# Causal attention scores on one core: mask and maximum of the second chunk in one VectorE instruction, normalisation on VectorE

## What is computed

```
x = _layernorm(x + causal attention 0 (x))        # 16 heads of 8
x = _layernorm(x + top-2 of 8 experts (x))        # relu
x = _layernorm(x + causal attention 1 (x))        # 16 heads of 8, low-rank q and k
x = _layernorm(x + F(x))                          # F: see below

def _layernorm(x, axis=-1, eps=1e-05):
    m = jnp.mean(x, axis=axis, keepdims=True)
    v = jnp.var(x, axis=axis, keepdims=True)
    return (x - m) / jnp.sqrt(v + eps)

attn = scale * jnp.einsum('bhqd,bhkd->bhqk', q, k)
causal = jnp.tril(jnp.ones((s, s), dtype=bool))
attn = jnp.where(causal[None, None], attn, -jnp.inf)
attn = jax.nn.softmax(attn, axis=-1)
ans = jnp.einsum('bhqk,bhkd->bhqd', attn, v)
```

## Time and profile before

| | us |
|---|---|
| median of 3 runs | 1263.61 |
| lowest and highest | 1262.74, 1264.56 |
| the profiled execution | 1266.6 |
| its span, first to last instruction | 1264.9 |
| TensorE matmul busy | 1131.2 (89%) |
| TensorE weight load busy | 611.5 (48%) |
| VectorE busy | 868.9 (69%) |
| ScalarE busy | 780.6 (62%) |
| GpSimd busy | 308.1 (24%) |
| mean granted clock of TensorE | 0.965 |

### The profile page before, as it was taken

One profiled execution on the slowest core, in us unless ns is written; L12 is line 12 of the kernel. 1 busy time (PEld: TensorE's weight loads), 2 busy tenths in 40 slices (PEclk: granted clock), 3 DMA queues, 4 the chain that ended last, 5 costly groups with the idle time before them and its releaser, 6 DMA issues. The chain is left out here.

```text
span 1264.9 us, 24994 instructions
## 1 busy us (share of the span) xinstructions
PE 1131.2 (89%) x8797; PEld 611.5 (48%) x8872; DVE 868.9 (69%) x2104; ACT 780.6 (62%) x1536; POOL 308.1 (24%) x839
## 2 busy tenths in 40 slices
PE   5899998999999988999878998788888888899996
PEld 3466675666766745666545532112112212126775
DVE  2888767772434486788747878769999888914344
ACT  4377656766443445676556656767887767884443
POOL 7234332522212113433243310211101101100001
PEclk9899999999999989999989988989999989999998
DMA  3444342110003400333211311101111000000000
GB/s 86 123 103 111 90 109 75 46 30 2 1 1 76 103 21 29 100 94 90 63 63 31 61 34 23 23 10 28 35 35 34 17 16 11 11 1 1 10 9 17
DMA packets 40058, 57.71 MB, mean 46 GB/s; under 512 B 9494, under 2 KB 15078, under 8 KB 39678
## 3 DMA queue, kind: packets, MB, share of 16 engines
q1 hardware_dynamic: 39934, 56.11, 18.1%
HBM read 30.81 MB, written 24.64 MB: 44 GB/s over the span
## 5 line engine op out<-in xcount | busy, mean ns | idle before, releaser
L842 ACT ACTIVATE probs<-bank 128x512 f32<-128x512 f32 x1088 | 574.3, 602 | 279.9 <-PE bank L1204 277.9
L941 DVE TENSOR_REDUCE tile_max<-bank 128x1 f32<-128x512 f32 (+3 forms) x1152 | 611.8, 592 | 75.5 <-PE bank L1189 71.0
L1189 PE MATMUL bank<-qk 100*128 100x128 bf16 (+2 forms) x1664 | 399.2, 318 | 79.4 <-DVE tile_max L941 60.5
L1204 PE MATMUL bank<-qk 128*128 128x128 bf16 (+4 forms) x1608 | 370.2, 311 | 7.7 <-ACT probs L842 7.2
L1233 PE MATMUL bank<-probs,v_head 128*32 128x512 f32 (+3 forms) x3328 | 310.9, 463 | 0.1
L1189 PEld LDWEIGHTS bank<-qk 100*128 100x128 bf16 (+1 forms) x1664 | 135.8, 98 | 329.7 <-DVE tile_max L941 244.6
L1112 DVE SCALAR_TENSOR_TENSOR acc<-bank,gate,acc 128x128 f32<-128x128 f32 x256 | 72.0, 344 | 154.6 <-PE bank L1362 154.5
L1233 PEld LDWEIGHTS bank<-probs,v_head 128*32 128x32 f32 x3328 | 141.7, 110 | 52.1 <-issue 30.3
L1204 PEld LDWEIGHTS bank<-qk 128*128 128x128 bf16 (+1 forms) x1664 | 135.7, 97 | 63.0 <-ACT probs L842 26.2
L935 DVE TENSOR_REDUCE tile_max<-bank 128x4 f32<-128x512 f32 x128 | 87.5, 687 | 91.0 <-PE bank L1189 90.9
L862 ACT ACTIVATE probs<-bank,sb_b 128x512 f32<-128x512 f32 x128 | 81.1, 684 | 109.9 <-PE bank L1351 109.8
(11 more groups left out here) (132 smaller groups left out, 655.9 us busy)
## 6 DMA issues: line engine op xcount, KB each, us to landing
qk<-qk_parts SPq DMA_DIRECT2D x160, 144.0 KB
qk_parts<-q_parts SPq DMA_DIRECT2D x48, 192.0 KB, 2.4
qk_parts<-k_parts SPq DMA_DIRECT2D x48, 192.0 KB, 3.1
qk_parts<-q_parts SPq DMA_DIRECT2D x24, 96.0 KB, 2.3
qk_parts<-k_parts SPq DMA_DIRECT2D x24, 96.0 KB, 2.9
sb_w<-in_w SPq DMA_DIRECT2D x8, 256.0 KB, 3.8
sb_w<-in_w SPq DMA_DIRECT2D x2, 1024.0 KB, 5.1
qk<-neg_rows SPq DMA_DIRECT2D x96, 6.0 KB
```

What stands on the lines that cost most here:

```text
L842: nc.scalar.activation(probs[:, hd.probs_place(c), :], S2[i % len(S2)][:], ACT.Exp, scale=hd.a.scale).then_inc(sem("probs"), 1)
L941: ins = nc.vector.tensor_reduce(tile_max[:, hd.slot, t, which:which + 1], s1[:, at:at + P * count], AX.X, ALU.max)
L1189: ins = mm(s1[:, at:at + P * count], qk[hd.query_rows, hd.place, 0, P * t:P * (t + 1)], qk[hd.query_rows, hd.place, 1, P * k0:P * (k0 + co ...
L1204: ins = mm(s2[:, at:at + P * count], qk[hd.key_rows, hd.place, 1, P * j:P * (j + 1)], qk[hd.key_rows, hd.place, 0, P * q0:P * (q0 + count) ...
```

## The change

- In chunk 1 of a causal head's scores by query, TensorE no longer writes the mask. VectorE takes each block of 128 columns in a `tensor_tensor_reduce`, which adds the mask, writes the sum back to PSUM and takes the maximum of the block. Chunk 0 stays as it was.
- A norm's root is computed on GpSimd, as (variance + eps) to the power -0.5, in two instructions. The normalisation runs on VectorE. ScalarE has no part in it.
- The rest of q and k (`second_rest`) comes after the third chunk of a batch on VectorE, not after the second.
- The extra rows with the maxima lie at partitions 61 to 63 and 125 to 127, not 36 to 38 and 100 to 102; the products by query take 125 or 61 rows, not 100 or 36. The rows between hold zeros.
- In the second attention output of attention 1 and the first routing of expert layer 1 the steps stand at other places.

```
-QUERY_ROWS = 100
+QUERY_ROWS = 61
...
-            self.query_rows = slice(0, QUERY_ROWS)
+            self.query_rows = slice(0, P // 2 + QUERY_ROWS)
...
-            self.query_rows = self.data_rows[0]
+            self.query_rows = slice(64 * half, 64 * half + QUERY_ROWS)
...
-place = put_attention_out(1, 1, at_head(65, 1), (0, 1, 2, 4, 6, 8, 9, 11, 12, 14))
+place = put_attention_out(1, 1, at_head(65, 1), (0, 2, 4, 6, 8, 10, 12, 15, 17, 19))
...
-put_routing(1, 0, put_attention_out(2, 0, at_head(82, 0), (0, 2, 4, 6, 8)), (0, 2, 4, 6, 8, 12, 14, 16, 18))
+put_routing(1, 0, put_attention_out(2, 0, at_head(82, 0), (0, 2, 4, 6, 8)), (0, 2, 4, 6, 10, 13, 15, 17, 19))
...
@@ GpSimd, between
-                    if kind == "norm":
-                        k, c = which
-                        pool.wait_ge(sem("rstd"), NORM_OF[(k, c)])
-                        for t in range(TPC * c, TPC * (c + 1)):
-                            ins = nc.gpsimd.tensor_scalar(x[:, t, :], x_plus[:, t, :], mean_var[:, t, 0:1],
-                                                          rstd[:, t:t + 1], ALU.subtract, ALU.mult)
-                        ins.then_inc(sem("normed"), 1)
+                    if kind == "root":
+                        k, chunks = which
+                        group = slice(TPC * chunks[0], TPC * (chunks[-1] + 1))
+                        pool.wait_ge(sem("var"), STATS_OF[(k, chunks[-1])])
+                        link(nc.gpsimd.tensor_scalar(rstd[:, group], mean_var[:, group, 1], LN_EPS, None, ALU.add))
+                        nc.gpsimd.tensor_tensor(rstd[:, group], rstd[:, group], minus_half[:, group], ALU.pow
+                                                ).then_inc(sem("rstd"), 1)
@@ ScalarE, between
-                    if kind == "root":
-                        k, chunks = which
-                        group = slice(TPC * chunks[0], TPC * (chunks[-1] + 1))
-                        act.wait_ge(sem("var"), STATS_OF[(k, chunks[-1])])
-                        nc.scalar.activation(std[:, group], std[:, group], ACT.Sqrt).then_inc(sem("std"), 1)
@@ VectorE, find_max
-                if a.query_diagonal(c):
+                if a.query_diagonal(c) and c == 1:
+                    for t in range(4):
+                        ins = nc.vector.tensor_tensor_reduce(
+                            out=s1[:, P * t:P * (t + 1)], in0=s1[:, P * t:P * (t + 1)], in1=mask16[:, t, :], scale=1.0,
+                            scalar=LOWEST, op0=ALU.add, op1=ALU.max, accum_out=tile_max[:, hd.slot, 4 * c + t, 0:1])
+                elif a.query_diagonal(c):
@@ VectorE, head
                         if c == batch[1] and before is not None:
                             between(before)
+                        if c == batch[2] and before is not None:
+                            rests(before)
@@ VectorE, statistics and norm
-                link(ins)
-                nc.vector.tensor_scalar(std[:, group], mean_var[:, group, 1], LN_EPS, None, ALU.add
-                                        ).then_inc(sem("var"), 1)
-
-            def inverse_root(k, c):
-                group = tiles(c)
-                dve.wait_ge(sem("std"), ROOT_OF[(k, c)])
-                nc.vector.reciprocal(rstd[:, group], std[:, group]).then_inc(sem("rstd"), 1)
+                ins.then_inc(sem("var"), 1)
+
+            def normed(k, c):
+                dve.wait_ge(sem("rstd"), ROOT_OF[(k, c)])
+                for t in range(TPC * c, TPC * (c + 1)):
+                    ins = nc.vector.tensor_scalar(x[:, t, :], x_plus[:, t, :], mean_var[:, t, 0:1], rstd[:, t:t + 1],
+                                                  ALU.subtract, ALU.mult)
+                ins.then_inc(sem("normed"), 1)
@@ TensorE, scores_by_query
-                if a.query_diagonal(c):
+                if a.query_diagonal(c) and c == 0:
                     mm(s1[:], ident16[:], mask16[:].rearrange("p t k -> p (t k)"), start=True, stop=False,
```

24 lines of the change are left out of this document (14 added, 10 removed).

## The result

The changed kernel takes **1242.05 us** (median of four runs, 1240.39 to 1242.97), where the one before takes 1263.62. The ratio is 0.9828, with a 95% interval of 0.9811 to 0.9845: 21.6 us or 1.7% faster. The profiled execution has a span of 1240.9 us, 24.0 less than before.

The account below looks back on a forecast made before the run. TensorE was taken as the bound in causal heads, with VectorE close behind, and VectorE from 900 to 1000 us. Gains of 23.6 us against a cost of 22.6 gave net -1, stated as 1262 us, range 1247 to 1286.

Parts of the forecast that it names:

- X: Time on VectorE from chunk 1's start to chunk 2's in a causal burst; taken as 1.16 us, bounds 0.80 to 1.40.
- part 5: Query products of 61 and 125 rows in place of 36 and 100: no cost, a possible gain left to rival (c).
- part 1: Chunk 1's mask moved from TensorE to VectorE: costs X - 0.82 us per burst, +22.6 us in all.
- Nothing behind the burst takes the delay back: Transpose of the maxima and products with V follow without a wait, so all 60 bursts pay 0.34 us: 20.4 us.
- the starts of the runs: First two heads of each causal run go at VectorE's pace, so chunk 1's added work costs 2.2 us there.
- Rival (a): Each read of chunk 1's maximum waits until its main instruction ends: X 1.48 to 1.84, 1284 to 1306 us; chance 0.17.
- rival (c): Shorter waits or more active rows keep the clock up from 720 to 870 us: 10 us gained, 1252; chance 0.18.
- Parts 2 and 3: Normalisation moves to VectorE (-9.6, -2, +2.2, end -2.3 us); root leaves ScalarE, saving table loads (-4.3 us).
- the tables' 4.3: TensorE's waits at four attention sites where ScalarE's table loads precede exponentials: 4.3 us gained without those loads.
- The end: Program's last norm: two small GpSimd instructions and 0.9 us on VectorE, 1.5 us instead of 3.85, so -2.3.
- Part 4: Rest of q and k one chunk later: -5.2 us in three causal bursts, -2.4 in four non-causal steps.
- Rival (b): Gains do not add up, as a removed wait meets the next step's: half the gains, net +11, 1274 us; chance 0.15.

## Why the prediction was wrong

Two steps failed. X was sized at 1.16 us and measured 0.96, which is 12.8 us of the sum. And part 5 stood in the sum at nothing, its effect on the clock set aside as a rival, where the rows alone brought 8 to 11 us. The other parts gave less than forecast.

**The mechanism of part 1 held, and its size did not.** TensorE's chunk 5 waits for VectorE's chunk 2, and the cost per burst is X - 0.82; the plain heads of the second attention grew by exactly that. "Nothing behind the burst takes the delay back" was wrong for every other head of the first attention, which did not grow, so the cost was met in full some 32 times and not 60. The term that was mis-sized is X: 1.16 by the prediction, 0.96 by the rows, because the read costs 0.04 and not 0.09; the 0.20 of the addition was right. 60 x 0.14 is 8.4 us in place of 20.4. With the starts of the runs (4 x 0.36) the sum had 22.6 and should have had 9.8. The experiments have 7 (undone) and 5 (alone), in keeping with 32 times 0.14 and the starts. The bound of 0.80 was fair and the measured value lay in the lower half of the range; a value of 1.16 "nearer the additions" rested on the gap behind a small reduction, which is not the same instruction. One number of the last part was a slip: the distance on TensorE should have read 1.17 + X, not 0.95 + X, since without the mask chunk 1's first product starts at 714.30 and not at 714.52; it does not enter the sum.

**Rival (a) is out.** The next main instruction starts 0.22 to 0.25 after one that lasts 0.30 to 0.33, and the read with it. The first rule of the Trainium skill's section ("VectorE: DVE Perf Modes", The DRAIN you can't avoid) would have given this rival's time; the trace does not agree. The section itself adds that an operation which is not held starts earlier, which the prediction left out. The same page's section "Two Vector instructions with no wait between them" counts the accumulator's read as an instruction of its own, and holds an instruction when its operands start in another group of 32 partitions than those of the instructions ahead. Here all operands span 128 partitions, so none is held, and with that the rows agree.

**The clock was counted as an alternative and belonged in the sum.** Part 5 was costed at nothing, which is right for the products themselves (386 ns for one of 61 rows and 399 for one of 36 in the earlier trace rows). Its effect was left to rival (c), with 0.18 and 10 us. Measured: some 36 of the 39 us at the lower level went away, and rows alone gave 11 us (8 when undone), 10.0 of them in heads 63 to 75 at some 30 us less of the lower level, so about 0.33 us for each us. The step that failed is the place of it, as one case among four and not as a term. The size of 10 us came near the 8 to 11 measured by luck: the quarter had no row, and it was nearly the whole of the 39 that left. TensorE's busy time in that stretch changed little (127.06 and 124.95 of 150 us, over more products), and its clock did.

**Parts 2 and 3.** Expected 9.6 + 2 - 2.2 + 2.3 + 4.3 = 16.0, measured 9 (5 to 12). The waits themselves went as said: 9.6 and 3.0 us for GpSimd are gone from the table, and 3.7 of the tables' 4.3. That the gain is 7 us smaller than their sum means that TensorE waited for something else in their place; which wait took how much stays open beyond the cases here. The expert layer and the last stage gave 5.9 and 1.3. The end was expected at -2.3 with 0.3 us for each GpSimd instruction, and 0.8 as the upper bound; the power takes 1.04, over both, and the end gave 1.3. Normalising costs VectorE 0.26 to 0.31 a tile, not 0.20, and eight in a row stood between chunk 1 and chunk 2, where the whole of them meets TensorE and not half.

**Part 4** was expected at -7.6 and measured at -4 to -6; the wait of 1.6 in each of three bursts went as said, and a part came back at the shared bank, for which the transpose of the maxima waited 0.35, 0.47 and 0.47 us. The prediction had overlooked that this transpose comes before the products with V. **The spacing** was nothing, as counted.

**Put together** by the runs, in us against the kernel before: mask +5 to +7, norm -9, rows -8 to -11, rests -4 to -6, spacing 0. They add up to between -14 and -21, and -21.6 was measured; each has an interval of 3 us or more, so the rest can be chance or effects of the parts on each other's clock. Against the forecast's -1, the mask is the larger error (some 16 us), the clock the next (8 to 11), and both went the same way; the norm (7) and the rests (2 to 4) went the other way and hid part of it. Rival (b), gains that don't add up, is thus half true of the norm and of part 4.

**The range** failed by how it was drawn: its low end was taken from rival (c) with X at 1.16, though the prediction itself gave -24 us for the low end of X. The two are independent, and together they reach 1230 (1262.6 less 23 and 10). A range over two large unknowns needs the corner where both go the same way, at least by half.

## What to carry to other kernels

Ask for each added instruction whether it stands between a product and the bank that the next product waits for, or ahead of the chunk for which the engine idles anyway: the same four pairs cost 5 to 7 us on chunk 1 and gave 4 to 8 on chunk 0. The same goes for steps slipped between two chunks, which cost less one chunk later: 4 to 6 us over the kernel. And where the granted clock is below 1.00 in a stretch, price it as a term of the sum, in us at the lower level, and add it to the end of the range instead of beside it.
